# A state-space scan fused with an MLP: GpSimd held back at five places, the last pair added by VectorE, one addition moved to ScalarE

## The reference, cut to what matters

```python
# the scan (d_inner 512, 16 states, 4 taps, rank 64)
xc, z = split(x @ in_proj_w.T)
xs = silu(causal_conv(xc, conv_w) + conv_b)
dt, B, C = split(xs @ x_proj_w.T)             # 64, 16, 16
dt = softplus(dt @ dt_proj_w.T + dt_proj_b)
h[t] = exp(dt[t] * A) * h[t-1] + dt[t] * B[t] * xs[t]     # A = -exp(A_log), h is 512 x 16
y[t] = sum over states (h[t] * C[t]) + D * xs[t]
out = (y * silu(z)) @ out_proj_w.T
# the MLP (ternary weights with a scale for each row)
h = silu(lin(x, w1)) * lin(x, w2)             # 1024 wide
h = gelu(lin(h, h1)); h = gelu(lin(h, h2))
out = lin(h, w3)
```

## Time and profile before

| | us |
|---|---|
| median of 3 runs | 4674.66 (4659.77 to 4681.23) |
| the profiled execution | 4663.26 |
| its span (first to last instruction) | 4661.1 |
| busy over the span: TensorE | 4014.4 (86%) |
| VectorE | 3460.9 (74%) |
| ScalarE | 2833.0 (61%) |
| GpSimd | 2099.1 (45%) |

### The profile page before, as it was taken

The page is one execution under the profiler, slowest core; times in us unless marked ns, Lnnn a source line. Parts: engine busy times, 40 slices in busy tenths (PEclk is TensorE's granted clock), DMA queues, the critical chain, the costliest instruction groups (busy, mean ns, idle before and its releaser), DMA issues. The chain is left out here.

```text
span 4661.1 us, 106603 instructions
## 1 busy us (share of the span) xinstructions
PE 4014.4 (86%) x39260; PEld 2163.3 (46%) x39268; DVE 3460.9 (74%) x5867; ACT 2833.0 (61%) x4496; POOL 2099.1 (45%) x1893
## 2 busy tenths in 40 slices
PE   7799999876768952499999999999988999999887
PEld 3344444553446720245444444444444545555554
DVE  7899999564544469898888988887026878888585
ACT  3477777553443235587787877876124766667563
POOL 4222222331233559887888888877000222222322
PEclk9899999897987975699999999999998999999998
DMA  4211111014322534365555655545213222222001
GB/s 126 81 38 37 37 37 39 14 44 96 69 97 83 130 105 104 89 170 133 143 144 137 165 142 144 145 137 158 73 62 121 59 66 55 57 62 62 30 1 37
DMA packets 263333, 411.34 MB, mean 88 GB/s; under 512 B 52332, under 2 KB 139452, under 8 KB 262756
## 3 DMA queue, kind: packets, MB, share of 16 engines
q1 hardware_dynamic: 256040, 387.22, 31.0%
q0 software_dynamic: 6912, 18.88, 1.7%
HBM read 351.85 MB, written 53.37 MB: 87 GB/s over the span
## 5 line engine op out<-in xcount | busy, mean ns | idle before, releaser
L1074 DVE CUSTOM_DVE_ANT_0 banks<-banks,l3s_table 128x1024 f32<-128x1024 f32 x512 | 620.1, 1240 | 126.5 <-PE banks L994 122.5
L1155 ACT ACTIVATE l3s_probs<-banks 128x512 f32<-128x512 f32 x1024 | 542.3, 595 | 256.3 <-PE banks L994 140.4
L2716 POOL TENSOR_TENSOR l_dbx<-l_u,l_bc 128x1024 f32<-128x1024 f32 x256 | 614.1, 2399 | 139.2 <-DVE banks L3096 107.8
L1069 DVE TENSOR_REDUCE l0s_peak<-banks 128x1 f32<-128x1024 f32 x512 | 605.1, 1213 | 59.4 <-PE banks L994 58.5
L1155 ACT ACTIVATE l0s_probs<-banks 128x512 f32<-128x512 f32 x1024 | 535.8, 601 | 174.6 <-PE banks L994 172.9
L2726 POOL TENSOR_TENSOR l_ys<-l_ys,l_hc 128x1024 f32<-128x1024 f32 x240 | 578.1, 2409 | 110.4 <-DVE l_hc L3107 106.3
L2928 ACT ACTIVATE banks<-l_dt,l_decay 128x512 f32<-128x512 f32 x512 | 346.3, 688 | 242.6 <-DVE banks L3096 238.6
L2844 PE MATMUL banks<-l_hb,l_ring 128*128 128x512 f32 x1024 | 445.4, 595 | 4.6 <-DMA l_ring<-in_l2f_stream 3.0
L2844 PE MATMUL banks<-l_ha,l_ring 128*128 128x512 f32 x1024 | 446.1, 593 | 0.0
L994 PE MATMUL banks<-l3s_q_st,l3s_k_st 122*32 122x512 bf16 x4096 | 354.0, 385 | 34.1 <-issue 23.6
L3096 DVE TENSOR_TENSOR_SCAN banks<-banks,l_carry,l_dbx 128x512 f32<-128x512 f32 x256 | 329.4, 1288 | 71.8 <-ACT banks L2928 44.3
(11 more groups left out here) (499 smaller groups left out, 7309.4 us busy)
## 6 DMA issues: line engine op xcount, KB each, us to landing
l_bc<-l_bc_rows SPq DMA_DIRECT2D x256, 512.0 KB, 5.5
l_ring<-in_l2f_stream SPq DMA_DIRECT2D x176, 512.0 KB, 6.6
l3s_table<-bias_tables SPq DMA_DIRECT2D x16, 960.0 KB
y_rows<-l1f_out_b SPq DMA_DIRECT2D x80, 128.0 KB, 1.7
qk_parts<-l0q_q_parts SPq DMA_DIRECT2D x48, 128.0 KB, 2.4
qk_parts<-l0q_k_parts SPq DMA_DIRECT2D x48, 128.0 KB, 2.4
l0s_q_st<-qk_parts SPq DMA_DIRECT2D x64, 96.0 KB
l0s_k_st<-qk_parts SPq DMA_DIRECT2D x64, 96.0 KB
```

Of the source, the lines that this page charges most:

```text
L1069: nc.vector.tensor_reduce(out=peak[:, b % 2, t:t + 1], in_=s1[t % 2], axis=AX, op=ALU.max, negate=True).then_inc(s1_used, 1)
L1074: nc.vector.tensor_tensor_reduce(out=s1[t % 2], in0=s1[t % 2], in1=rows, scale=1.0, scalar=LOW, op0=ALU.add, op1=ALU.max, accum_out=peak[: ...
L1155: nc.scalar.activation(columns(probs[b % 2][:, t, :], half * 512, (half + 1) * 512), scores, ACT.Exp, scale=scale).then_inc(s2_used, 1)
L2716: nc.gpsimd.tensor_tensor(dbx[:, at:at + 2], u[:, 2 * mh:2 * mh + 2], bc[:, load % BR, 0].unsqueeze(1).to_broadcast([P, 2, TB]), ALU.mult)\
```

## The change

- **GpSimd is held** at five places of its loop over pairs: before the product of pair 1 until `gated` of the block before has made half 1 (`y_ready`); before pair 8 until `remainder` of half 1 has ended (a new semaphore `softened`); before pair 12 until `step_size` of half 1 has ended; before pair 25 until `gated` of half 0 has ended; before pair 30 until `remainder` of the next block's half 0 has ended.
- **The last pair** (31) of a block is no longer added to `ys` by GpSimd: `gated` of half 1 first adds it from `hc` to `xs` on VectorE, then waits for GpSimd's sum of pair 30. The semaphore counts (`ADDS`, `sums_to`) follow.
- **`gated` of half 1** moves from step 0 of the next block to step 63 of its own.
- **`one_plus`** loses its first operation, which ScalarE now makes at the end of `soften` (Identity with bias 1), and is called `remainder`; it waits for `one_ready` instead of `exp_ready`.
- **`step_size`** moves from steps 59 and 19 to 60 and 20.

```diff
--- before.py
+++ after.py
@@ -2471,12 +2471,12 @@
     "xs": [35, 38, 40, 46],
     "gelu": [32, 35, 38, 42, 44, 47, 49, 50, 58, 59, 61, 62, 63, 5, 11, 11],
     "xp": 49,
-    "gated": [46, 0],
+    "gated": [46, 63],
     "post_stats": 5,
     "pre_l_stats": 9,
     "pre_stats": 12,
-    "one_plus": [56, 12],
-    "step_size": [59, 19],
+    "remainder": [56, 12],
+    "step_size": [60, 20],
     "scale_out": [14, 14],
     "post_l_stats": 16,
     "up": [17, 17, 18, 19, 20, 21, 21, 23],
@@ -2513,7 +2513,7 @@
     UNITS = states * CT
     HALF = UNITS // 2
     PAIRS = UNITS // 2
-    ADDS = PAIRS - CT // 2
+    ADDS = PAIRS - CT // 2 - 1
     LAG = 3
     MAIN = 2 * HT - LAG
     AT = FUSED
@@ -2561,6 +2561,7 @@
         abs_done = s.sem("abs_done")
         exp_ready, one_ready, ln_ready = s.sem("exp_ready"), s.sem("one_ready"), s.sem("ln_ready")
         dt_ready, u_ready = s.sem("dt_ready"), s.sem("u_ready")
+        softened = s.sem("softened")
         da_ready, dbx_ready, h_ready, hc_ready = (s.sem(n) for n in ("da_ready", "dbx_ready", "h_ready", "hc_ready"))
         add_done, y_ready = s.sem("add_done"), s.sem("y_ready")
 
@@ -2636,7 +2637,7 @@
             if k < 0:
                 return sums_to(n - 1, k + UNITS) if n else 0
             mh, r = divmod(k, HALF)
-            return n * ADDS + mh * (HALF // 2 - 1) + r // 2
+            return n * ADDS + min(mh * (HALF // 2 - 1) + r // 2, ADDS)
 
         def tokens(n):
             return chip.x[:, n * BT:(n + 1) * BT, :]
@@ -2719,7 +2720,7 @@
 
             def pair_sum(n, i):
                 mh, st = divmod(i, HALF // 2)
-                if st:
+                if st and i < PAIRS - 1:
                     wait(g, hc_ready, n * UNITS + 2 * i + 2)
                     wait(g, add_done, sums_to(n, 2 * i - 1))
                     at = 2 * i % CR
@@ -2737,6 +2738,16 @@
             for n in range(NB + 2):
                 b, b2 = n - 1, n - 2
                 for i in range(PAIRS):
+                    if i == 1 and n < NB:
+                        wait(g, y_ready, 2 * n)
+                    if i == AT["remainder"][1] // 2 + 2 and n < NB:
+                        g.wait_ge(softened, 2 * n + 2)
+                    if i == AT["step_size"][1] // 2 + 2 and n < NB:
+                        g.wait_ge(u_ready, 2 * n + 2)
+                    if i == AT["gated"][0] // 2 + 2 and n < NB:
+                        g.wait_ge(y_ready, 2 * n + 1)
+                    if i == AT["remainder"][0] // 2 + 2 and n + 1 < NB:
+                        g.wait_ge(softened, 2 * n + 3)
                     if n < NB:
                         pair_product(n, i)
                     if i < 2 and 0 <= b < NB:
@@ -2950,6 +2961,8 @@
                         .then_inc(taken[bank], 1)
                 act.wait_ge(abs_done, n * CT + 2 * half + 2)
                 nc.scalar.activation(ea[:, at], ea[:, at], ACT.Exp, scale=-1.0).then_inc(exp_ready, 1)
+                act.wait_ge(exp_ready, 2 * n + half + 1)
+                nc.scalar.activation(eb[:], ea[:, at], ACT.Identity, bias=1.0).then_inc(one_ready, 1)
 
             def logarithm(n, half):
                 act.wait_ge(one_ready, 2 * n + half + 1)
@@ -3036,9 +3049,14 @@
 
             def gated(n, half):
                 mine = xs[n % 2]
-                v.wait_ge(add_done, sums_to(n, (half + 1) * HALF))
                 v.wait_ge(skip_done, n * CT + 2 * half + 2)
                 at = slice(2 * half, 2 * half + 2)
+                if half:
+                    v.wait_ge(hc_ready, (n + 1) * UNITS)
+                    last = (UNITS - 2) % CR
+                    nc.vector.tensor_tensor(mine[:, at], mine[:, at], hc[:, last:last + 2], ALU.add)
+                    v.drain()
+                v.wait_ge(add_done, sums_to(n, (half + 1) * HALF) if not half else (n + 1) * ADDS)
                 nc.vector.tensor_tensor(mine[:, at], mine[:, at], ys[:, at], ALU.add)
                 moved(v, f"z{n}.{2 * half + 1}")
                 v.drain()
@@ -3067,16 +3085,14 @@
                     last = nc.vector.tensor_tensor(scaled[:, 2 * i + k, :], banks[:, bank, k * D:(k + 1) * D], so[:], ALU.mult)
                 last.then_inc(taken[bank], 1)
 
-            def one_plus(n, half):
+            def remainder(n, half):
                 at = slice(2 * half, 2 * half + 2)
-                v.wait_ge(exp_ready, 2 * n + half + 1)
-                nc.vector.tensor_scalar(eb[:], ea[:, at], 1.0, None, ALU.add).then_inc(one_ready, 1)
-                v.drain()
+                v.wait_ge(one_ready, 2 * n + half + 1)
                 nc.vector.scalar_tensor_tensor(out=ea[:, at], in0=eb[:], scalar=-1.0, in1=ea[:, at],
                                                op0=ALU.add, op1=ALU.subtract)
                 moved(v, f"dt{n}.{2 * half + 1}")
                 v.drain()
-                nc.vector.tensor_tensor(ea[:, at], u[:, at], ea[:, at], ALU.subtract)
+                nc.vector.tensor_tensor(ea[:, at], u[:, at], ea[:, at], ALU.subtract).then_inc(softened, 1)
 
             def step_size(n, half):
                 at = slice(2 * half, 2 * half + 2)
@@ -3122,7 +3138,7 @@
                 convolve(0, c)
             v.wait_ge(decay_exp, 1)
             nc.vector.tensor_scalar(decay[:], decay[:], -1.0, None, ALU.mult)
-            one_plus(0, 0)
+            remainder(0, 0)
             step_size(0, 0)
             for n in range(NB + 2):
                 b, b2, more = n - 1, n - 2, n + 1 < NB
@@ -3134,8 +3150,8 @@
                         if k + 1 < UNITS:
                             scan(n, k + 1)
                         times_c(n, k)
-                    if k == AT["gated"][1] and have:
-                        gated(b, 1)
+                    if k == AT["gated"][1] and n < NB:
+                        gated(n, 1)
                     if k == AT["post_stats"] and have:
                         for i in range(2):
                             moved(v, f"y{b}.{i}")
@@ -3145,8 +3161,8 @@
                         pre_l.statistics(v, lambda t: tokens(b)[:, t, :])
                     if k == AT["pre_stats"] and more:
                         pre.statistics(v, lambda t: tokens(n + 1)[:, t, :])
-                    if k == AT["one_plus"][1] and n < NB:
-                        one_plus(n, 1)
+                    if k == AT["remainder"][1] and n < NB:
+                        remainder(n, 1)
                     if k == AT["step_size"][1] and n < NB:
                         step_size(n, 1)
                     for i in range(2):
@@ -3163,8 +3179,8 @@
                             convolve(n + 1, i)
                     if k == AT["gated"][0] and n < NB:
                         gated(n, 0)
-                    if k == AT["one_plus"][0] and more:
-                        one_plus(n + 1, 0)
+                    if k == AT["remainder"][0] and more:
+                        remainder(n + 1, 0)
                     if k == AT["step_size"][0] and more:
                         step_size(n + 1, 0)
```

## The result

| | before | changed |
|---|---|---|
| median, us | 4676.04 (4 runs, 4659.77 to 4681.23) | 4611.0 (4 runs, 4601.51 to 4617.24) |
| the profiled execution | 4663.26 | 4617.24 |
| its span | 4661.1 | 4615.2 |

The ratio is 0.9862, 95% interval 0.9838 to 0.9886: 65 us less; 4600 in a range of 4572 to 4645 was forecast. The two profiled executions differ by 46 us only, and that must be understood before their traces are compared: the first scan begins at 1734.9 us in the one and at 1750.9 in the other, behind code that nobody touched. From the first scan to the last block's `outputs` the traces show 1517.5 and 1454.8 us, 62.7 less; what follows takes 1408.6 and 1409.5.

What follows compares the result with a forecast made beforehand. VectorE's chain to y_ready was taken to end the 194.4 us period; terms of 9.0 us gave 185.4, and 67 us over the stage took 4663.3 to 4596, put at 4600, range 4572 to 4645.

Steps and rivals of the forecast that it cites:

- Half 0 gate: At step 46, the gate's second operation falls from 3.22 to 1.23 us, the first keeps its 2.19: 2.0 us a period.
- Last pair and gate: At a block's end, VectorE adds the last pair and gates in three operations of 1.23 us: 2.0 us saved a period.
- TensorE earlier against ScalarE: ScalarE's waits for TensorE at steps 11 and 12 go, so VectorE's scans wait less: 2.0 us a period (0 to 3).
- step_size of half 0: Moved to step 60, behind the GpSimd sum that it met: 1.2 us a period taken, between 0 and 2.5.
- step_size of half 1: Moved to step 20, where GpSimd's residual addition, which no hold keeps back, falls: 0 taken, between 0 and 2.0 us.
- ScalarE's two additions: ScalarE takes over the additions of 1, 2.2 us of its 41 us idle: 0.8 us a period charged (0 to 2.3).
- the value set on line 3073: In half 0 at step 56, the operation leaves VectorE, 2.37 us and a 0.1 gap, within 2.6 us taken for remainder.
- First block: Without MLP: 3.1 us from earlier y_ready, 2.3 from a wait and a collision, 8 from the holds: 13 us.
- GpSimd as the pace: Rival: holds use up GpSimd's idle time and it sets the period, 8.1 us longer: 4728 us, chance 0.05.
- The holds miss: Rival: GpSimd is behind when VectorE arrives, operations still meet, 3.6 us a period left: 4634 or 4640 us, chance 0.21.
- Given back: Rival: VectorE's time turns into waits for ScalarE and late weights: 4650 to 4665 us, chance 0.09.
- TensorE's floor: Rival: the period reaches TensorE's own 183.0 us without new waits: 4580 us, chance 0.09.

Runs made afterwards that it cites:

- e5: The kernel before with a quarter of the MLP's hidden products left out: 4625.7 us in one run, 191.8 us a period.
- e2: The kernel before with only four of the holds of GpSimd added, all but the one at pair 1: 4645.9 us, ratio 0.9934 to the kernel before.
- e4: The changed kernel with the addition of 1 back on VectorE and off ScalarE: 4611.3 us, ratio 0.9864 to the kernel before.
- e6: The changed kernel with a quarter of the MLP's hidden products left out: 4580.0 us in one run, 185.4 us a period.
- e9: The changed kernel with the output products' copy, the statistics and the norm's small operations moved to earlier steps: 4600.9 us, ratio 0.9850 to the kernel before.
- e10: The changed kernel with earlier statistics, third hold before the MLP's residual addition, residual steps moved, addition of 1 on VectorE: 4599.5 us, ratio 0.9844 to the kernel before.
- e1: The changed kernel without its five holds of GpSimd: 4647.8 us, ratio 0.9944 to the kernel before.

## Why the prediction was right, and where it was not

**The bound of before** was VectorE's chain, as said: taking 19 us of work off TensorE changed its period by 2.6 of 194.4 us (e5), while the holds alone, which touch nothing but GpSimd's waits, changed it by 2.7 (e2) and the whole change by 8.4.

**The terms of a period.** To place the gain I took the starts of scans 2, 9, 16, 47, 56, 60 and 63, mean of four blocks in each trace:

| stretch of a block | before | changed | gain | terms forecast there |
|---|---|---|---|---|
| scan 2 to 9 | 17.5 | 17.5 | 0 | |
| 9 to 16 | 28.9 | 27.1 | 1.8 | 2.0 and 0 |
| 16 to 47 | 86.4 | 86.5 | -0.1 | 0 |
| 47 to 56 | 24.6 | 24.1 | 0.5 | 2.0, less 0.8 |
| 56 to 60 | 14.5 | 12.5 | 2.0 | 2.6 |
| 60 to 63 | 10.9 | 8.6 | 2.3 | 1.2 |
| 63 to scan 2 of the next | 11.5 | 9.6 | 1.9 | 2.0 |
| sum | 194.4 | 186.0 | 8.4 | 9.0 |

*Half 0 gate*: right to the tenth on VectorE (3.22 to 1.23, 2.18 stays). *Last pair and gate*: 1.9 for 2.0. *remainder of half 1* and *step_size of half 1*: nothing for nothing, the latter for the reason given, the residual addition. *TensorE earlier against ScalarE*: 1.8 for 2.0, and that is the mean of two kinds: 2.6 in the periods without a fall of the clock (26.3 us) and 1.0 in those with one (27.9). *step_size of half 0*: 2.3 where I took 1.2 of 0 to 2.5. Between scans 47 and 60 the terms were 3.8 us together and the traces show 2.5. So that the sum came out at 8.4 for 9.0 is in part luck: step_size gave 1.1 more, and the clock and ScalarE took more than was charged.

**The term that failed** is "ScalarE's two additions", charged with 0.8 us because "nothing but 0.8 us of waits stands behind them", and with it the value set on line 3073. ScalarE's idle time (41 us a period) was no cover, for it lies elsewhere: from 2446.5 to 2470 us of the changed trace, right behind the addition, ScalarE goes from table loads of 1.28 us to gelus to exponentials with no wait that the trace lists. The waits of VectorE for ScalarE between scans 47 and 63 grew from 1.6 to 4.7 us; e4 shows that 1.9 of this growth hangs on the moved addition, which gave VectorE 1.5 in `remainder`. The rest, 1.2, was there without it; that it came because VectorE arrives sooner is argued, not shown. Of the 3.4 us that `remainder` of half 0 lost on VectorE (5.67 to 2.25), 2.0 are the hold's, since line 3091 stays at 1.23 with the addition back (e4), and only these lasted.

**The ceiling.** I wrote that "both ledgers meet": VectorE's and TensorE's round would tie. They do: the wait before `outputs` is 0. But what TensorE newly waits for is not what I named. Late weights hold it no longer than before (0.5 us a period); the 3.0 us above the floor of 183.0 are 1.7 of wait for ScalarE ahead of dt, 0.3 ahead of z, and 1.1 of lower clock, less 0.1. And the tie does not make TensorE's work the bound: e6, with 20 us less of it, still takes 185.4, and e9 and e10 show that moving the work of the other engines goes on paying down to 183.3. The chain that is left runs through the engines in turn, TensorE's products between `outputs` and gate and up among them, as the lower clock there shows by lengthening the period.

**First block**: 9.7 for 13, and the second period 5.7 for 7. I had let every hold give its steady value there; without an MLP GpSimd is further behind, and in the first block lines 3095 and 3101 still meet it (3.20 and 2.59 us at its end). The third period gave 11.4 for 9: before, its scans 16 to 24 took 32.0 us against some 29 in the later periods, and after the change 28.7; why they were slower there is open.

**The rivals.** GpSimd as the pace: no, it is idle for 29.7 us of 186.0 and the scans' wait for it did not grow. The holds miss: no (e1, 37 us). Given back: in part, 3.1 us a period to ScalarE between scans 47 and 63. Of the last two, TensorE's floor was not reached by the change, but by e10.

**The rule of the Trainium skill** ("SBUF — State Buffer", section "Who interferes with whom") that a meeting blocks one side for a whole instruction agrees with every trace (an operation of 1.23 us that meets a whole one of GpSimd takes 3.1 to 3.4). That a hold only moves the wait to GpSimd is also what happened: 24.9 us of its idle time in four periods end with line 3063. It cost nothing, because GpSimd had 33 us a period of idle time and VectorE stood on the chain.

## What to carry to other kernels

Two engines that exclude each other share one time budget: give it to the one on the chain, with a wait on the other placed one operation ahead of each group, and look whether an operation just outside the hold still meets it. Before you move work to an engine because its sum of idle time is large, look at what is queued there in the stretch behind the move. A wait that has shrunk to zero in front of an engine doesn't make that engine the bound: take work off it and see, and look whether its clock stayed the same when you do. Where the clock is granted at two levels, split the periods by it before you compare means.

## What the runs showed that I had not expected

GpSimd's tiny operations of 128 x 4 wait for VectorE's like large ones: line 1443 takes 0.20 us elsewhere and 1.19 on average where it falls beside `remainder` (groups of the changed kernel; before, beside line 3073, 0.56).

```profile
L1443 POOL TENSOR_TENSOR l2n_pre_rstd<-l2n_pre_mean_var,eps 128x4 f32<-128x4 f32 x4 | 4.8, 1190 | 0.0
```

And code that is the same in all fourteen profiles took 1732.6 to 1750.9 us until the first scan: 18 us, more than most single edits here are worth, which is why the stretches of the traces were compared and not their spans. The granted clock goes with the time as well: the four runs of the changed kernel took 4617.2, 4612.9, 4609.1 and 4601.5 us at a mean clock of 0.927, 0.928, 0.930 and 0.931.
